# Two routed adapter layers: loops that turn inside a step, a reordered GpSimd program and another order of the first loads

## The reference

```python
def layer(adapter, x, W_down, b_down, W_up, b_up, g, b):      # W_down (3,1024,512), W_up (3,512,1024)
    h = einsum('bsh,bhk->bsk', x, W_down[adapter]) + b_down[adapter][:, None, :]
    h = gelu(h, approximate=False)
    y = x + einsum('bsk,bkh->bsh', h, W_up[adapter]) + b_up[adapter][:, None, :]
    mean = y.mean(-1);  var = ((y - mean) ** 2).mean(-1)
    return (y - mean) * rsqrt(var + 1e-5) * g[adapter][:, None, :] + b[adapter][:, None, :]
out = layer(adapter, layer(adapter, x, *weights_0), *weights_1)
```

## Time and profile before

| | us |
|---|---|
| three runs, median | 2846.11 |
| the profiled execution, its own time | 2846.24 |
| its span, first to last instruction | 2844.5 |
| PE busy | 2707.2 |
| DVE busy | 2168.6 |
| ACT busy | 1699.4 |
| POOL busy | 1362.8 |

### The profile page before, as it was taken

One profiled execution on the slowest core, in us unless ns is written; L12 is line 12 of the kernel. 1 busy time (PEld: TensorE's weight loads), 2 busy tenths in 40 slices (PEclk: granted clock), 3 DMA queues, 4 the chain that ended last, 5 costly groups with the idle time before them and its releaser, 6 DMA issues.

```text
span 2844.5 us, 57001 instructions
## 1 busy us (share of the span) xinstructions
PE 2707.2 (95%) x11714; PEld 2219.5 (78%) x11714; DVE 2168.6 (76%) x3325; ACT 1699.4 (60%) x2907; POOL 1362.8 (48%) x952
## 2 busy tenths in 40 slices
PE   6799999998899999999989999999889999999996
PEld 4588888887688888888768878888767878888885
DVE  2677777776776777777888877878788878778886
ACT  2566666655666666656656665666555656556564
POOL 0454545554554545454454444444354444444446
PEclk8899999999999999999999999999999999999999
DMA  5465656667566666656666656656666666566663
GB/s 155 160 214 196 216 199 215 202 206 229 184 210 206 207 209 205 212 200 216 213 202 213 215 193 195 222 187 218 197 208 202 207 195 219 188 198 212 211 197 144
DMA packets 366521, 574.37 MB, mean 202 GB/s; under 512 B 41472, under 2 KB 241280, under 8 KB 365952
## 3 DMA queue, kind: packets, MB, share of 16 engines
q1 hardware_dynamic: 364224, 563.32, 60.9%
q0 software_dynamic: 1728, 6.29, 0.7%
HBM read 364.97 MB, written 204.47 MB: 200 GB/s over the span
## 4 chain that ended last, share of the span: by engine, by line
PE 71%; issue 14%; POOL 4%; DVE 4%; POOLq 2%; ACT 2%; DVEq 1%; ACTq 1%; SPq 1%; DMA 0%
PE pD L477 37%; PE bX L489 18%; PE bZ L489 15%; DVE wul L751 1%; DVEq L215 1%; POOL rstd L415 1%; POOLq L449 1%; DVE xt L836 1%; POOL cs L432 1%; POOLq L215 1%; ACT pC L638 1%; POOL cs L430 1%; ACTq L215 1%; ACT xh L587 1%; DVE hl L818 0%
## 5 line engine op out<-in xcount | busy, mean ns | idle before, releaser
L422 POOL TENSOR_TENSOR xt<-xt,cgb 128x1024 f32<-128x1024 f32 x260 | 663.6, 2554 | 495.6 <-ACT xt L646 495.6
L477 PE MATMUL pD<-wdh,xh 128*128 128x512 f32 x2080 | 818.9, 394 | 71.4 <-DVEq L780 71.2
L477 PE MATMUL pD<-wdl,xh 128*128 128x512 f32 x2080 | 815.6, 392 | 0.0
L477 PE MATMUL pD<-wdh,xl 128*128 128x512 f32 x2080 | 815.4, 392 | 0.0
L477 PEld LDWEIGHTS pD<-wdh,xh 128*128 128x128 f32 x2080 | 394.0, 189 | 165.2 <-DVEq L780 68.3
L859 DVE SCALAR_TENSOR_TENSOR xt<-xt,nmean,cgb 128x1024 f32<-128x1024 f32 x260 | 468.2, 1801 | 0.0
L477 PEld LDWEIGHTS pD<-wdh,xl 128*128 128x128 f32 x2080 | 394.2, 190 | 82.6
L477 PEld LDWEIGHTS pD<-wdl,xh 128*128 128x128 f32 x2080 | 394.3, 190 | 81.2
L430 POOL TENSOR_TENSOR cs<-hT 128x256 f32<-128x256 f32 x130 | 97.6, 750 | 727.8 <-DVE hT L803 721.8
L489 PE MATMUL bX<-wuh,hh 128*128 128x512 f32 x1040 | 408.7, 393 | 34.0 <-DVE xt L828 20.6
L489 PE MATMUL bX<-wul,hh 128*128 128x512 f32 x1040 | 406.5, 391 | 0.0
(11 more groups left out here) (91 smaller groups left out, 3748.0 us busy)
## 6 DMA issues: line engine op xcount, KB each, us to landing
xq<-in_xB SPq DMA_DIRECT2D x130, 512.0 KB, 3.8
htok<-hg SPq DMA_DIRECT2D x260, 256.0 KB, 2.8
hq<-htok SPq DMA_DIRECT2D x1040, 64.0 KB, 2.2
xt<-in_x SPq DMA_DIRECT2D x130, 512.0 KB, 4.2
mid<-xt SPq DMA_DIRECT2D x130, 512.0 KB, 4.1
xq<-mid SPq DMA_DIRECT2D x520, 128.0 KB, 3.2
xt<-mid SPq DMA_DIRECT2D x130, 512.0 KB, 4.3
out<-xt SPq DMA_DIRECT2D x130, 512.0 KB, 3.2
```

What stands on the lines that cost most here:

```text
L422: eng.tensor_tensor(xt[:, k, :], xt[:, k, :], cgb[:, 1, :], ALU.add).then_inc(s_o, 1)
L477: last = eng.matmul(pD[e][:, :], a[:, e, 128 * k:128 * k + 128], w[:, k, :], start=False, stop=(k == 7 and n == 2), skip_group_check=True)
```

## The change

1. **DVE's and ACT's loops** run `end(i-1)` and then `begin(i)` (`halves`), so that the jump back lies inside a step. On DVE `begin` ends with `low_h(w, 0)` and `end` begins with `onto(u, 3)`; on ACT `begin` ends with the branches for `take_wu_2` and `take_wd_1`, and `end` begins with `high_h(w, 1)`.
2. **Order inside the step.** DVE: `onto(u, 2)` moves ahead of `take_wu_2`, `take_wd_1` and both `ready`; `onto(u, 3)` ahead of `variance` and `scale(., 0)`. ACT: `take_wu_2` and `take_wd_1` move behind `high_x`, `gelu`, `seed_d` and `high_h(., 0)`.
3. **POOL:** `take_bu` moves from the end of a step to behind `sums` and `norm` of the next; the first `take_gb` moves from the start of the kernel to its place in the step. T4 goes from DVE's `take_wu_1` to POOL's `factors`.
4. **First loads:** the first half of W_down comes in 4 DMAs, not 8, with one semaphore for both quarters; ACT waits for b_down behind `high_wd`, not ahead of it; the first W_up is asked for in step -1, not in step 1. `seed_z`, no longer `seed_x`, waits for `s_cb` (it comes first in ACT's order).

```diff
+        def halves(begin, end):
+            def body(i):
+                end(i + -1)
+                begin(i)
+            return body
...
+            def first_half(row, c):
+                eng.wait_ge(f_rd, c * 4 + 2)
+                for a in range(4):
+                    eng.dma_start(rwd[32 * a:32 * a + 32, :, :, :].rearrange("p q c n -> p (q c) n"),
+                                  Wd[row, 256 * a:256 * a + 128, :].rearrange("a (k i) n -> (a i) k n", i=32))\
+                       .then_inc(s_rd[0], 16)
...
             def first_weights(p):
                 row, c = adapter(p), pd1.next()
-                quarter(row, c, 0)
-                quarter(row, c, 1)
+                first_half(row, c)
...
                 load_rows(w, 0)
                 load_rows(w, 1)
-                when_new(eng, v, up_weights)
+                if not v.first():
+                    when_new(eng, v, up_weights)
...
                 when_new(eng, i + 1, down_rest)
+                if (i + 1).first():
+                    up_weights(i + 1)
...
                 eng.tensor_tensor(b11, b12, b11, ALU.subtract).then_inc(s_sub, 1)
+                eng.wait_ge(s_wul, c * 7 + 3)
+                eng.tensor_tensor(b12, b21, b12, ALU.subtract).then_inc(s_sub, 1)
...
-            take_gb(Pair(0))
-
             def step(i):
-                u, w, v = i + -3, i + -2, i + -1
+                u, w = i + -3, i + -2
                 sums(w)
                 norm(u + -1)
+                if w.exists():
+                    when_new(eng, w, take_bu)
+                    eng.drain().then_inc(s_cb, 1)
                 shift(u + -1, 0)
                 when_new(eng, w, factors)
                 shift(u + -1, 1)
                 if u.exists():
-                    if not u.first():
-                        when_new(eng, u, take_gb)
+                    when_new(eng, u, take_gb)
                     eng.drain().then_inc(s_cg, 1)
-                if v.exists():
-                    when_new(eng, v, take_bu)
-                    eng.drain().then_inc(s_cb, 1)
...
             def take_wd_0(p):
                 c = pd[0].next()
-                eng.wait_ge(s_bd, c * 16 + 16)
                 high_wd(p, c, 0)
                 high_wd(p, c, 1)
+                eng.wait_ge(s_bd, c * 16 + 16)
+                eng.sem_inc(s_seen, 1)
...
-            def step(i):
-                u, w = i + -3, i + -2
-                when_new(eng, u, take_wu_2)
+            def begin(i):
                 high_x(i, 1)
-                when_new(eng, i, take_wd_1)
                 gelu(i + -1, 1)
                 seed_d(i, 1)
-                high_h(w, 0)
+                high_h(i + -2, 0)
+                when_new(eng, i + -3, take_wu_2)
+                when_new(eng, i, take_wd_1)
+
+            def end(i):
+                u, w = i + -3, i + -2
                 high_h(w, 1)
                 when_new(eng, w, take_wu_0)
...
-            steps(eng, step, -1, NPH + 4)
+            steps(eng, halves(begin, end), -1, NPH + 5)
...
                 low_wu(c * 7, 3, b22)
-                eng.wait_ge(s_sub, c * 4 + 3)
-                eng.tensor_tensor(b12, b21, b12, ALU.subtract).then_inc(s_sub, 1)
...
-            def step(i):
+            def begin(i):
                 u, w = i + -3, i + -2
-                X = bX[u.c % 2]
                 transpose_h(w, 0)
                 transpose_h(w, 1)
-                onto(u, 1, X, 0, 0)
+                onto(u, 1, bX[u.c % 2], 0, 0)
                 low_x(i, 1)
+                onto(u, 2, bZ, 1, 1)
                 when_new(eng, u, take_wu_2)
                 ready(u, s_wu[2])
                 when_new(eng, i, take_wd_1)
                 ready(i, s_wd[1])
-                onto(u, 2, bZ, 1, 1)
                 low_h(w, 0)
+
+            def end(i):
+                u, w = i + -3, i + -2
+                X = bX[u.c % 2]
+                onto(u, 3, X, 0, 1)
                 variance(u + -1)
                 scale(u + -1, 0)
-                onto(u, 3, X, 0, 1)
                 transpose_x(i + 1, 0)
                 low_h(w, 1)
...
-            steps(eng, step, -1, NPH + 4)
+            steps(eng, halves(begin, end), -1, NPH + 5)
```

8 lines of the change are left out of this document (4 added, 4 removed).

## The result

The changed kernel took 2823.1 us (median of four runs, 2819.0 to 2828.8); the kernel before took 2846.6 beside it. The ratio is 0.992, with a 95% interval of 0.9897 to 0.9943. Five more runs of it, beside nine of the kernel before on the same chip, gave 2822.6 against 2845.5, ratio 0.9921 (0.9907 to 0.9934). So the change gains 23 us, not 58. The forecast had the sign; the time lies 9 us above its range.

What follows compares the result with a forecast made beforehand. The prediction took PE to bound the kernel nearly everywhere, at 0.2267 us a matmul, other engines mattering only where PE stands. Turns -14, start -22 and changes -22 gave -58 from 2846.24: 2788 us, range 2768 to 2814.

Steps and rivals of the forecast that it cites:

- Start: Steps 0 to 3: earlier first loads and W_up cut the loss from 62.5 to about 40 us, -22 (bounds -14, -27).
- Turns: Loop turns in the steady stretches: moved inside the step, they cut the loss from 23.6 to 10 us, -14.
- Changes: The three changes of adapter, pairs 30, 65 and 95: shorter PE waits, together -22 us (bounds -8, -34).
- Product 5's wait, -1 for each: Step 32 at a change: second wuh made when it is now, PE's wait shrinks from 2.6 to about 2, -1.
- Product 2's wait 3.45 to 1.7: Step after T1's at each change: T2 later but taken behind the seeds, T4 off DVE; PE's wait falls to about 1.7.
- D02, -1 for each: At each change: ACT's high_x goes ahead of take_wu_2, so PE's wait before D02 falls by 1 us.
- New W_down, -10.5 in three steps: Steps with new W_down: turn, b_down wait and SP issues go; -4.5 at pair 30, -1 at 65, -5 at 95.
- The rule that I set aside: DVE and POOL block each other on SBUF: wul beside T4 grows up to 3 us a change, 9 in all; sum 2797.
- Rival 5: Early loads only move the wait, changes of adapter stay, the turns alone gain: 2822 us; chance 0.06.
- Rival 2: DVE becomes late behind its turn in layer 1, product 6 waits, turns cost 21 as now: 2799 us; chance 0.15.
- Rival 3: POOL blocks on b_up's load, T2, seeds and shifts 3.4 us late at all four changes: +14, 2802; chance 0.14.
- Rival 6: Every step: branches behind onto(u, 2) outlast their 0.7 us cover, so the kernel gets slower, 2895 us; chance 0.05.

## Why the prediction was wrong

**Start: -22 forecast, -14 to -15 measured.** The first matmul comes 4.9 to 5.8 us earlier (5.8 to 6 forecast) and product 0 of step 3 at 66 us (66.1, 65.7), as forecast. The step that failed is "In step 3 the wait for product 2 goes too". That wait grew: it is 6.1 and 5.5 us where it was 2.7. D02's wait is 4.6, so "about 5 us stay" held, but the lower clock behind it was left out; D02's group loses 7.5, as before (7.4). In all step 3 loses 15.0 and 14.4 where about 5 were forecast. T2 waits there for b_up's load and its subtraction (2.08 and 2.24 us), DVE's low_h next to T4 took 2.50 us, not 0.69, and D02 stood behind take_wu_2. With T1 to T4 small the wait for product 2 is nearly gone (1.2 lost), and with take_wd_1 first D02's is (1.7 lost).

**Turns: -14 forecast, -5 to -7 measured.** The mechanism of the forecast is seen: waits before products 5 and 6, none on `ready`. Its size is off: 1.9 us a turn in layer 1, where 1.2 was said, and 0.2 to 0.6 in layer 0 where none was. The deeper fault is the credit. I priced the turn's new place as the gain; the new order alone gives 17 in layer 1, and the new place takes some 7 back.

**Changes: -22 forecast, nothing measured.** This is the larger failure. Its steps are "product 5's wait shrinks from 2.6 to about 2" and "product 2's wait falls from 3.45 to about 1.7": neither wait moved (2.63 and 3.40). Term by term:
- *Product 5's wait, -1 for each.* Nothing came: 2.63 us for 2.62. I had written down that variance runs 2.4 us later, and priced T1 at 9.6 us into the step (it was 10.5). Onto 4 starts 15.7 us into step 32, and started at 15.6: it waited behind late sums, and waits behind a late T1. What I didn't do was to ask what the same part gives without that delay: 10 us, as the kernel with POOL's part alone shows.
- *Product 2's wait 3.45 to 1.7.* It stayed at 3.40. I held the b_up load as harmless up to 5 us. But T2 waits for T1, b_up and a shift in turn; moving T1 some 3 us ahead gave 6.5 us back in two experiments.
- *D02, -1 for each.* This came: the wait fell from 5.77, 6.61 and 6.03 us to 4.50, 4.65 and 4.64, and D02's groups lose 3.3 less over the three steps (ACT's old order gives 2.8 of it back). It didn't last: product 2's groups lose up to 0.7 more, the groups at product 3 some 2 more. And D02 stands behind take_wu_2 in both kernels. I named that queue ("it keeps the three `wuh` and three `wul` of `take_wu_2`") and didn't ask why D02 has to stand in it. That one order is worth 22 us, as much as the whole change.
- *New W_down, -10.5 in three steps.* They lose 2.5 to 4 more. The turn of pair 30 left product 2 (3.6 us in step 30 became 0.5), but in its new place it costs 2 us ahead of the first down quarter, as the kernel with turns between steps shows. And D02 loses 3.4 more over the three steps, of which ACT's order (take_wd_1 behind gelu, the seed and high_h) holds 2.4.
- *T4 on POOL at no cost.* In the changes it is equal on both engines: 1.22 us off DVE, 0.9 (step 33) to 1.8 (step 3) back as low_h beside T4. In step 3 it costs 1 to 2 us.
- *The end, within 1.* It gained 1.9 us.

**The rule that I set aside.** I had found two POOL rows next to DVE work that differ by 0.9, and left the rule inside the range. The 9 us that it gave for `wul` beside T4 didn't come; `wul` had started first. The larger meetings are with T1 and T3, which I hadn't priced. The rows now say more: `scale` 1.27 alone and 3.60 beside a T1 of 2.41; low_h 0.69 alone and, in the changed kernel, 2.94 beside a T3 of 2.41 (timelines of DVE and of POOL):

```profile
708.79 2.94 DVE L834 TENSOR_TENSOR hl<-cs,hh 128x512 fp32r<-128x512 f32 x1 [1.50 <-issue]
```

```profile
708.77 2.41 POOL L417 TENSOR_TENSOR rwu<-rwu 128x1024 f32<-128x1024 f32 x1
```

When both start together DVE's instruction takes its own time plus POOL's. When it starts later, it takes its own plus what is left of POOL's: low_h that started 1.05 us ahead of T4's end took 1.60. Of the 153 instructions of `scale`, `low_h`, `low_x` and `wul` in the changed kernel that start while a POOL instruction of over 2 us runs, 151 fit this within 0.3 us. The other way round POOL waits for DVE's: T4 takes 3.30 beside `wul` (the others 2.4 alone), and the power 1.68 beside `scale`, 0.70 without. So in these rows POOL loses at most some 1.2 us, the length of DVE's instruction, and DVE up to 2.4; the rows that I used show POOL's side. Onto, which reads one of its two inputs from PSUM, takes 0.68 beside a whole `shift` of POOL's. The Trainium skill (SBUF — State Buffer, Who interferes with whom) calls the shared port pair an exclusive lock, and these runs agree. How much of the 17 to 19 us of the small factors is this and how much is POOL's own time, no run tells apart.

**The rivals.** Rival 5's number, 2822, is what came, at a chance of 0.06, and by luck. Its story is half right: the changes stay, but the early loads gain 14 to 15 and the turns 5 to 7, not 10. Rival 2 (2799) described the waits at layer 1's turns, at some three quarters of its size (15 us lost for 21). Rival 3 blamed a slow load of b_up; it landed in 5.96 us, at the fast end, and still stood in T2's way. Rival 6 is out: quiet steps are 20.40 us to the hundredth. The range failed since all its cases but rivals 5 and 6 held a gain of 8 us and more in the changes.

## What to carry to other kernels

When two parts of a change touch one chain of waits, price each on the other's order, not both on the old one: variance moved by one part was the releaser of T1 moved by the other. When a wait on a semaphore is long, ask first what stands ahead of the increment on its engine that has nothing to do with it; exchanging two blocks did as much here as the whole change. And when work goes to POOL beside a DVE that PE waits for, price it on DVE: an instruction of DVE's can grow by the whole of POOL's (1.27 us to 3.60 beside 2.41).
